# Projection carried into the attention loop piece by piece, with a new order of the products within a step

## The reference, cut to what matters

```python
mod = silu(c) @ wmod                          # shifts, scales and gates per batch
h = layernorm(x) * (1 + ca) + sa
q, k, v = split(h @ qkv_w.T)                  # 16 heads, 16 dimensions each
soft = tanh(h @ hex_w.T); code = tanh(h @ q6_w.T)
scores = alpha * tanh(q k^T / beta) + lam * soft soft^T / 2 + lattice(code, code)
out = softmax(causal(scores)) @ v ; x = x + ga * (out @ out_w.T)
h = layernorm(x) * (1 + cb) + sb              # then top 2 of 8 experts, each silu(h w1 + b1) w2 + b2
x = x + gb * sum_of_weighted_experts
```

## Time and profile before

| | us |
|---|---|
| median of 3 runs (lowest to highest) | 2136.32 (2136.0 to 2142.38) |
| the profiled execution's own time | 2131.18 |
| its span | 2129.3 |
| modulation, until DMA and engines of the projection start | 44.9 |
| projection, and attention's first loads | 222.0 |
| attention, first product to last | 1056.5 |
| output, then router with its end | 79.0 and 181.6 |
| experts | the rest, about 545 |

### The profile page before, as it was taken

One profiled execution on the slowest core, in us unless ns is written; L12 is line 12 of the kernel. 1 busy time (PEld: TensorE's weight loads), 2 busy tenths in 40 slices (PEclk: granted clock), 3 DMA queues, 4 the chain that ended last, 5 costly groups with the idle time before them and its releaser, 6 DMA issues. The chain is left out here.

```text
span 2129.3 us, 37498 instructions
## 1 busy us (share of the span) xinstructions
PE 1857.6 (87%) x10466; PEld 1188.4 (56%) x10467; DVE 1214.2 (57%) x2548; ACT 1283.8 (60%) x1387; POOL 357.8 (17%) x383
## 2 busy tenths in 40 slices
PE   2988199899898999999979998869809999999997
PEld 1433054444444444444434443758709999999997
DVE  5544167677676777777757776667512332332332
ACT  4332089899898998989979998124303223223222
POOL 1321200000100000000000000413541222222222
PEclk7989589999999999999989999889959999999999
DMA  3455680603406033150530600571236666666663
GB/s 125 144 172 183 170 182 18 131 10 76 81 16 136 5 86 71 34 118 5 102 55 21 131 11 22 155 237 61 74 138 191 188 177 180 189 175 178 189 176 86
DMA packets 156588, 239.43 MB, mean 112 GB/s; under 512 B 17697, under 2 KB 90273, under 8 KB 156385
## 3 DMA queue, kind: packets, MB, share of 16 engines
q1 hardware_dynamic: 142400, 218.50, 38.1%
q0 software_dynamic: 13824, 19.03, 4.5%
q10 hardware_dynamic: 288, 1.08, 0.2%
HBM read 173.53 MB, written 65.03 MB: 112 GB/s over the span
## 5 line engine op out<-in xcount | busy, mean ns | idle before, releaser
L771 DVE SCALAR_TENSOR_TENSOR probs<-probs,scal,bil_ps 128x512 f32<-128x512 f32 (+1 forms) x1152 | 773.6, 715 | 278.3 <-ACT probs L734 183.3
L734 ACT ACTIVATE probs<-raw_ps 128x2048 f32<-128x2048 f32 (+1 forms) x288 | 518.8, 1801 | 83.5 <-PE raw_ps L669 83.5
L741 ACT ACTIVATE probs<-probs 128x2048 f32<-128x2048 f32 (+1 forms) x288 | 529.8, 1839 | 34.9 <-DVE probs L771 34.8
L681 PE MATMUL bil_ps<-u_mv,w_st 128*128 128x512 f32 (+3 forms) x1280 | 469.9, 426 | 54.3 <-DVE probs L771 31.1
L681 PEld LDWEIGHTS bil_ps<-u_mv,w_st 128*128 128x128 f32 x1280 | 217.1, 192 | 411.3 <-DVE probs L771 380.1
L1429 ACT ACTIVATE hid_t<-fc_ps,b 128x128 f32<-128x128 f32 x576 | 156.7, 383 | 414.8 <-PE fc_ps L1396 235.9
L669 PE MATMUL raw_ps<-q_mv,k_st 128*128 128x512 f32 (+3 forms) x1280 | 335.9, 389 | 50.9 <-DMA v_sb<-v_rows 43.1
L696 PE MATMUL o_ps<-probs,v_sb 128*32 128x512 f32 (+3 forms) x2560 | 299.7, 550 | 0.4 <-POOL probs L654 0.4
L669 PEld LDWEIGHTS raw_ps<-q_mv,k_st 128*128 128x128 f32 x1280 | 211.1, 193 | 142.4 <-ACT probs L734 69.8
L1396 PE MATMUL fc_ps<-rows_t,w 128*128 128x128 f32 x2304 | 271.5, 276 | 0.0
L1396 PEld LDWEIGHTS fc_ps<-rows_t,w 128*128 128x128 f32 x2304 | 265.5, 193 | 0.1
(11 more groups left out here) (183 smaller groups left out, 1196.4 us busy)
## 6 DMA issues: line engine op xcount, KB each, us to landing
w<-in_w SPq DMA_DIRECT2D x80, 1024.0 KB, 6.1
q_mv<-q_split SPq DMA_DIRECT2D x128, 128.0 KB
rows<-x_rows SPq DMA_DIRECT2D x72, 130.0 KB, 2.3
v_rows<-v_st SPq DMA_DIRECT2D x8, 1024.0 KB, 5.0
k_st<-k_split SPq DMA_DIRECT2D x64, 128.0 KB
k_st<-k_split SPq DMA_DIRECT2D x128, 64.0 KB
v_sb<-v_rows SPq DMA_DIRECT2D x32, 256.0 KB
o_t<-o_sb SPq DMA_DIRECT2D x32, 256.0 KB, 2.2
```

What stands on the lines that cost most here:

```text
L681: mm = pe.matmul(bil_ps[:, hd % 2, column:column + width], w_st[:, kt * P:(kt + 1) * P], u_mv[:, hd, qb * BLK + query:qb * BLK + query + w ...
L734: act.activation(probs[:, s % NBUF, :, first:BLK], raw_ps[:, :, first:BLK], ACT.Tanh).then_inc(tanh_ready, 1)
L741: act.activation(scores, scores, ACT.Exp).then_inc(exp_ready, 1)
L771: dve.scalar_tensor_tensor(scores, scores, scal[:, ALPHA:ALPHA + 1], bil_ps[:, hd % 2, first:BLK], ALU.mult, ALU.add).then_inc(sum_ready, 1)
```

## The change: what it does

`stage_projection` and `stage_attention` become one stage, `stage_front`. The blocks of 512 tokens are taken in the order batch 0 block 0, batch 1 block 0, batch 0 block 1 and so on; for each block the four head groups are attended (32 iterations of 3, 7, 11 or 15 steps, again 288 steps in all), all of it written out without loops. The first two blocks are projected ahead of attention (`HEAD_PARTS`). The other six are cut into parts (two transposes T0 and T1, codes C, Q0 to Q3, lattice L, V0, V1, guard G), and most parts into two halves; a table (`SLOT`) gives each piece to a step, where PE issues it between the bias products of heads 2, 3 and those of heads 0, 1. All pieces share one PSUM bank (`part_ps`), which DVE empties between its second and third sum of the next step. The splits of these six blocks move to POOL, as do their layer norm's scale and shift; modulation no longer normalises x.

```diff
-def diagonal_steps(qb):
+BLOCKS = [(i % B, i // B) for i in range(N_BLK)]
+ITERS = [(i, g) for i in range(N_BLK) for g in range(NG)]
...
+PARTS = ["T0", "T1", "C", "Q0", "L", "Q1", "Q2", "V0", "Q3", "V1", "G"]
+EARLY = 2
...
+        step = max(OPENS[i] + n * (CLOSES[i] - OPENS[i]) // len(PIECES), taken + (half != 1))
+        SLOT.setdefault(step, []).append((i, o, half))
```

```diff
                     for hd in range(HG):
+                        row = hd % 2 * ROWS
                         mm = pe.matmul(raw_ps[:, hd, column:column + width],
-                                       k_st[:, hd // 2, kt * P:(kt + 1) * P],
-                                       q_mv[:, hd, qb * BLK + query:qb * BLK + query + width],
-                                       start=True, stop=True)
+                                       k_st[row:row + ROWS, p, hd // 2, kt * P:(kt + 1) * P],
+                                       q_mv[row:row + ROWS, p, hd // 2, query:query + width], start=True, stop=True)
```

The order in a step of PE's loop:

```diff
-                    if at(s + PE_LEAD):
-                        raw_scores(*at(s + PE_LEAD))
-                    if at(s + PE_LEAD - 1):
-                        bilinear(*at(s + PE_LEAD - 1), LAST_TWO)
-                    weighted_values(it, s)
-                    if at(s + PE_LEAD):
-                        bilinear(*at(s + PE_LEAD), FIRST_TWO)
+                if s + PE_LEAD < NSTEP:
+                    raw_scores(s + PE_LEAD)
+                weighted_values(s)
+                if s + PE_LEAD - 1 < NSTEP:
+                    bilinear(s + PE_LEAD - 1, (2, 3))
+                for i, o, half in SLOT.get(s, []):
+                    project(i, o, half)
+                if s + PE_LEAD < NSTEP:
+                    bilinear(s + PE_LEAD, (0, 1))
```

On POOL, then on DVE, then on SP ahead of the steps:

```diff
+            for s in range(NSTEP):
+                if s in MASKS_BEFORE:
+                    mask(s)
+                for i, o in DONE_AT.get(s - POOL_LAG, []):
+                    if o == "C":
+                        split_codes(i)
...
+                for i, t in NORM_AT.get(s, []):
+                    normalise(pool, then_wait, i, t)
...
+                for hd in range(HG):
+                    if hd == HG // 2:
+                        for i, o in DONE_AT.get(s - 1, []):
+                            if o != "C":
+                                empty(i, o)
+                    if s + DVE_LEAD < NSTEP:
+                        score_sum(s + DVE_LEAD, hd)
...
+            for o in ("Q0", "C", "Q1", "Q2", "L", "Q3"):
+                store(0, o)
+            load_keys(0)
+            store(0, "V1")
...
+            load_values(1)
+            for o in ("Q0", "C", "Q1", "Q2", "L", "Q3", "V1"):
+                store(1, o)
```

```diff
-            pool.wait_ge(pads_ready, 1)
-            for e in range(E):
-                pool.indirect_dma_start(dram["x_rows"], bass.IndirectOffsetOnAxis(ap=pad_row[:, e:e + 1], axis=0),
-                                        blank[:, :], None).then_inc(scattered, 16)
+            for e in range(E):
+                row = sp.value_load(pad_row[0:1, e:e + 1], min_val=0, max_val=VOID)
+                sp.dma_start(dram["x_rows"][ds(row, P), :], blank[:, :]).then_inc(pads_stored, 16)
```

More of the change, by code:

```diff
@@ L224, in _ @@
             act.activation(rstd[:, :], rstd[:, :], ACT.Sqrt).then_inc(std_ready, 1)
-            act.wait_ge(shift_ready, 1)
-            for n in range(NTILE):
-                tile = x_sb[:, n * D:(n + 1) * D]
-                act.activation(tile, tile, ACT.Identity, bias=shift[:, n:n + 1], scale=rstd[:, n:n + 1])
         @block.tensor
@@ new lines, in emptied_before, with multiplied, part_rows @@
+        def emptied_before(eng, part):
+            n = PART_NUMBER[part]
+            last = n - (N_EARLY if n < len(HEAD_PARTS) else 1)
+            if last >= 0:
+                i, o = PART_ORDER[last]
+                if o == "C":
+                    eng.wait_ge(code_ready, i + 1)
+                else:
+                    eng.wait_ge(emptied, EMPTIED[i, o])
+        def multiplied(eng, i, o):
+            eng.wait_ge(part_mm, PART_NUMBER[i, o] + 1)
+        def part_rows(name, sides, parts, n, side, part, b, c):
+            view = dram[name].rearrange("(z h q r) t -> z h q r t", h=sides, q=parts, r=n)
+            return view[b:b + 1, side, part, :, c * BLK:(c + 1) * BLK].rearrange("z h r t -> (z h) r t")
@@ new lines, in mask @@
+            def mask(s):
+                pool.wait_ge(exp_ready, s + 1)
+                for _, column, _, _ in STEPS[s][1]:
+                    tri = probs[:, s % NBUF, :, column:column + P]
+                    ins = pool.affine_select(out=tri, in_=tri, compare_op=ALU.is_ge, fill=0.0, base=0,
+                                             pattern=[[0, HG], [1, P]], channel_multiplier=-1)
+                ins.then_inc(mask_ready, 1)
+            split_codes(0)
+            split_lattice(0)
+            split_guard(0)
@@ L753, in _ @@
-            with act.Fori(0, NIT - 1) as it:
-                iteration(it, False)
-            iteration(NIT - 1, True)
+            for i in range(EARLY):
+                make_codes(i)
+                for m in range(4):
+                    high_half(i, m)
+            tanh(0)
+            for s in range(NSTEP):
+                if s + 1 < NSTEP:
+                    tanh(s + 1)
+                exp(s)
+                for i, o in DONE_AT.get(s - 2, []):
+                    if o == "C":
+                        make_codes(i)
```

878 lines of the change are left out of this document (500 added, 378 removed).

## The result

The changed kernel takes 2226.47 us (median of 4 runs, 2218.19 to 2236.45) where the one before takes 2136.16 in the same runs: ratio 1.0433, interval 1.0399 to 1.0467. It is 4.3% slower; the forecast of 2010 us, faster, was wrong by 216. Its profiled execution took 2230.17 us, 222 more than the working's 2008. A ratio leaves out executions over 1.5% above the fastest of their kernel (e2, e4, e6 and e11 have such), a median does not.

What follows compares the result with a forecast made beforehand. It took ACT to bound attention before the change, then a PE-DVE ring of 3.90 us a step. 2131.2 less 106 (attention) and 17 (later stages) gave 2008, 2013 at the median's level, stated as 2010; range 1925 to 2100.

Steps and rivals of the forecast that it cites:

- Step 1: Full attention step: weighted values enter the PE-DVE ring, halves run side by side; 3.90 us a step, 0.34 longer.
- 5: Rest of attention, from step 21's exp: 242 full steps of 3.90 and 25 short of 2.5, 944 + 62 us.
- the ring of 3.90: Attention's cycle: head 1's bias product, raw scores, weighted values, head 2's bias product, two DVE sums; 3.90 us.
- step 2: Attention's 32 short steps of 256 columns: by the same ring about 2.5 us each.
- step 6: Attention's masks behind POOL's splits: late masks hold up PE, 8 us, bounds 0 and 40.
- (a): Rival for attention: ring under 3.56, ACT stays the bound; 1916 us, chance 0.12.
- (b): Rival for attention: the array's halves don't run side by side, 4.46 per full step; 2159 us, chance 0.10.
- Rival (d): Rival for the written-out program: fetching its instructions stalls the engines; left out, given no chance of its own.
- Step 3: Projection pieces on PE within attention: half a part takes 0.89 us, hidden except where both halves share a step, 3 us.
- Step 4: Head of the stage: SP's queue sets the pace; PE starts steps at about 96, step 21 at 197 us.
- rival (c): Rival for the head: slower SP queue and POOL's splits cost 60 to 70 us more; 2075 us, chance 0.17.
- Step 8: Later stages: moved split of `rw1` gains 7 us, padding scatters leaving POOL 10; sum 17.

Runs made afterwards that it cites:

- e2: Changed kernel with raw scores over all 128 rows and every bias product over rows 0 to 49; 2569.06 us, ratio 1.1934.
- e4: Changed kernel with three useless 128-row products added in each of the 81 steps behind the last piece; 2134.45 us.
- e6: Changed kernel with one useless 128-row product added in each of the 81 steps behind the last piece; 2154.85 us.
- e11: Changed kernel with three useless products over 16 rows added in each of the 81 steps behind the last piece; 2236.71 us.
- e7: Changed kernel with three useless products added in the steps behind the last piece and in 55 earlier steps without a piece; 2101.75 us.
- e9: Changed kernel, its order and pieces kept, with every raw and bias product over all 128 rows; 2176.72 us, ratio 1.021.
- e13: Changed kernel with bias products over the 64 rows of their half instead of 50; 2165.96 us, ratio 1.0161.
- e10: Kernel before with weighted values ahead of the bias products of heads 2 and 3, and bias products over 50 rows instead of 128; 2871.68 us.
- e15: Changed kernel with the new order only in steps with a piece, and bias products over 64 rows instead of 50; 2012.05 us.
- e5: Kernel before with the new order alone: weighted values ahead of the bias products of heads 2 and 3; 2317.24 us.
- e3: Kernel before with only its raw scores over 64 rows instead of 128; 2135.6 us, ratio 0.9994.
- e8: Changed kernel with the new order only in steps with a piece, the old order in the others; 2062.98 us.

## Why the prediction was wrong

**The step that failed is 1, and with it 5: the ring of 3.90 was priced at one clock.** All its terms came from rows at full clock, and 242 x 3.90 used it for all of attention. I had seen the columns of granted clock at 1.00 and treated them as given. From step 21's exp (233.9) to the end of attention the profile has 1195 us where the working has 1020: 175 of the 222 missing, nearly all of it the clock's (step 2 below has 14 of them, and step 6 gives 8 back). At full clock the step is 3.89; the mean from step 24 on is 4.45 at a mean clock of 0.78. Shown by e4, e7 and e9: with the same order and the clock held, steps take what the ring says. Shown by e13: rows of zeros, which change no result and leave the step at full clock as it was, raise the clock; e11 and, with a slightly longer ring, e10 show the same of rows left out.

I valued the halving of the rows for letting products run side by side, and charged nothing for it. That gain was measured: the ring is 4.36 with 128 rows (e9) and 3.89 without. The bill was larger: e9 at 4.36 beats the changed kernel by 50 us.

**Point by point.** *Step 1:* right at full clock, by 0.01; rivals (a) and (b) are out, ACT is idle 0.21 ahead of an exp and the halves do run side by side. Rival (d) is out as well: e15 runs the same written-out program with ACT busy in 280 of 288 us. The drain at a change of mode, the rule of the Trainium skill, page "TensorEngine Tiling (Array Packing)", Key Properties, that spoke against the change, costs the changed kernel nothing beyond the terms: head 1 and four raw products, up to the start of the weighted values, take 0.89 where 0.93 was allowed. Where products over 50 and over 128 rows take turns (e10), the trace agrees with the rule, with 0.2 us a step. *Step 2:* wrong at full clock too. No distance of two exps is near 2.5; the four around the diagonal take 3.76, 3.58, 3.85 and 3.58 (at full clock, 8 to 16 of each from step 24 on), 14.8 together where the working has 3 x 3.90 + 2.5 = 14.2. In 25 iterations that is 14 us. *Step 3:* right at full clock: steps with and without a piece take 3.85 alike. The half piece is 1.12, not 0.89, and still hidden. (The 114 of this term are pieces, and they stand in 108 steps: two share a step six times, not seven.)
```profile
681.72 1.12 PE L749 MATMUL part_ps<-rows_sb 128*128 128x512 f32 x2
681.82 2.96 DVE L937 SCALAR_TENSOR_TENSOR probs<-probs,scal,bil_ps 128x512 f32<-128x512 f32 x4 [1.08 <-PE bil_ps L797]
```
*Step 4:* the queue was well read and the head was still 37 us late: exp of step 0 at 104, of step 21 at 233.9, against 96 and 197. Block 0's first store, its first keys, block 1's first store and the keys of iteration 2 stand in SP's queue at
```profile
62.70 0.73 SPq L498 DMA_DIRECT2D q_split<-qk_hi  x1
84.35 1.27 SPq L532 DMA_DIRECT2D k_st<-k_split  x3
107.00 0.62 SPq L498 DMA_DIRECT2D q_split<-qk_hi  x1
127.95 3.83 SPq L532 DMA_DIRECT2D k_st<-k_split  x3
```
The forecast had the first keys issued by 84 (88.9 here), block 1's stores from 101 (107.0), iteration 2's keys near 120 (127.95). PE's waits from 104 to 234 us:
```profile
PE raw_ps L780 <- DMA q_mv<-q_split: 14.9, 3, 13.1
PE o_ps L816 <- issue: 6.1, 1, 6.1
PE o_ps L816 <- POOL probs L703: 5.1, 2, 3.3
PE part_ps L758 <- DVE qk_f L912: 4.6, 1, 4.6
```
The 13.1 is the wait for iteration 2's keys (16 forecast), so rival (c) holds in part. The 6.1 is the first product of an iteration's weighted values, at 218.4, while the DMA engines are full (share 1.03 from 214 to 234). The profile names no releaser, but the load of these values was issued at 214.69 and took 9.7 us to land, and the product starts at 224.52. The clock has its part again, 0.74 in this stretch. No run took the head apart, so the split of the 37 stays open. *Step 6:* from 256 us on PE waits 0.3 us for masks, not 8; the 5.1 above fall into the head. *Step 8:* 7 us came of 17. The output stage gained some 5, of 7 (72.8 us up to 1396.2 before, 67.6 up to 1496.6 now): the first `gated` now waits 0.39 instead of 9.60. The padding rows gained 9.6 of 10. But between the output stage and the router's first product, and in the router's products, the changed kernel loses 3.5 and 6.1. First the kernel before, then the changed one: router start, products, scatters.
```profile
1396.20:1419.30 23.10, 3.58 (x16) 3.19 (x17) 16.39 (x67) 2.29 (x4) 1.44 (x2) 0.62 0.70 229
1419.30:1533.70 114.40, 111.45 (x911) 92.93 (x909) 67.75 (x265) 50.76 (x75) 39.16 (x40) 0.99 0.34 112
1533.70:1594.50 60.80, 5.95 (x85) 4.83 (x85) 16.13 (x97) 1.19 (x4) 31.07 (x32) 0.56 0.33 121
```
```profile
1496.60:1523.20 26.60, 3.55 (x16) 3.15 (x17) 19.93 (x67) 2.41 (x4) 7.78 (x4) 0.55 0.70 229
1523.20:1643.70 120.50, 112.44 (x910) 92.84 (x909) 67.80 (x265) 49.98 (x75) 39.32 (x40) 0.99 0.21 71
1643.70:1694.90 51.20, 6.02 (x86) 4.90 (x85) 15.93 (x97) 1.19 (x4) 23.70 (x24) 0.56 0.39 141
```
POOL's 7.78 at the router's start are the split of `rw1`, moved and not gone. Where the 6.1 went was not settled. Nor is the 7 sharp: behind attention the old later stages took 814.7, 812.8 and 823.9 us (e5, e10, e3) where the new ones took 807.7, 802.3 and 804.8 on the same chips (e8, e9, e4), a gain of 7 to 19.

Sum of the misses in the two profiled executions: head 37, attention from step 21 on 175, later stages 10: 222.

**What stays open.** The runs show that rows in use and idle time both act on the clock, not by what law. That e15 came out at the 2010 us forecast for another kernel is partly chance: its steps are shorter (3.65) than forecast and its head is as late as the changed kernel's.

## What to carry to other kernels

Price a ring at both levels of the clock, and ask of every change to TensorE's work what the engine does less of: idle time and narrower products both count. Zeros that pad an operand to the full array cost no time in a product (0.50 us over 50 rows and over 128) and may hold the clock, so cutting them out is not free; where products must be narrow, pad them to the whole of their half. Compare steps of one kind at one clock before you say what a step costs. If the granted clock falls after a change, put useless full-height products into a wait that nothing stands behind: if the kernel gets faster, the clock is the cause.

## What the hardware showed that was not expected

- Bias products over 50 rows instead of 128, all else alike: 2317 to 2872 us, 4.36 to 4.54 us a plain step at full clock, granted clock 0.99 to 0.59 (e5, e10).
- Three useless products a step over 128 rows: 92 us faster; over 16 rows: no faster (e4, e11: 2134 and 2237 us, against 2226).
- 64 instead of 50 rows, 14 of them zeros: 55 us of attention in the changed kernel (e13), 43 in the mixed order (e15 against e8), with the step at full clock unchanged.
- Products in different halves of the rows run side by side: head 1 and four raw products 0.89 us from start to the next group's start, against 1.35 over 128 rows (e5) and 1.56 where 50 and 128 rows take turns (e10).
